# A quantised attention stage: 8-bit codes written as bytes into zeroed 16-bit words and multiplied as fp16, instead of codes raised by 1024 and copied to bf16

## The reference

```python
def _fq(x, delta, zp, n_bits):
    xi = round(x / delta) + zp
    xq = clip(xi, 0.0, 2.0 ** n_bits - 1.0)
    return (xq - zp) * delta
sim  = einsum('bhid,bhjd->bhij', _fq(q, dq, 128, 8), _fq(k, dk, 128, 8)) * SCALE
attn = softmax(sim, axis=-1)
out  = einsum('bhij,bhjd->bhid', _fq(attn, dw, 0.0, 8), _fq(v, dv, 128, 8))
```

## Time and profile before

| what | value |
|---|---|
| median of 3 runs | 1576.75 us |
| profiled execution, its own time | 1576.92 us |
| span of its records | 1575.1 us |
| VectorE busy | 1098.1 us |
| TensorE busy (matmul) | 1092.8 us |
| ScalarE busy | 894.2 us |
| GpSimd busy | 681.1 us |
| mean granted TensorE clock, share of full speed | 0.826 |

### The profile page before, as it was taken

One profiled execution on the slowest core, in us unless ns is written; L12 is line 12 of the kernel. 1 busy time (PEld: TensorE's weight loads), 2 busy tenths in 40 slices (PEclk: granted clock), 3 DMA queues, 4 the chain that ended last, 5 costly groups with the idle time before them and its releaser, 6 DMA issues.

```text
span 1575.1 us, 28607 instructions
## 1 busy us (share of the span) xinstructions
PE 1092.8 (69%) x9344; PEld 593.3 (38%) x9344; DVE 1098.1 (70%) x3102; ACT 894.2 (57%) x2546; POOL 681.1 (43%) x1055
## 2 busy tenths in 40 slices
PE   2888888887788797855353545444358778888888
PEld 1333344444333286831120212222225435453545
DVE  2687777777688653678888999877765666666522
ACT  1555554555554464567676797988852344646531
POOL 3321011011011416558888888877741344445310
PEclk9899999999999998975555555555569799999989
DMA  5213142101331112267555576665530121201000
GB/s 184 61 53 92 51 129 75 54 24 50 99 106 49 42 39 82 57 160 122 99 104 109 106 130 115 121 109 106 109 57 14 27 48 35 49 21 43 1 0 27
DMA packets 265219, 116.53 MB, mean 74 GB/s; under 512 B 216936, under 2 KB 253936, under 8 KB 262896
## 3 DMA queue, kind: packets, MB, share of 16 engines
q1 hardware_dynamic: 260112, 108.29, 30.8%
q0 software_dynamic: 2048, 4.20, 0.9%
q10 hardware_dynamic: 2912, 2.22, 0.5%
HBM read 38.80 MB, written 16.45 MB: 35 GB/s over the span
## 4 chain that ended last, share of the span: by engine, by line
PE 35%; POOL 21%; DVE 18%; issue 14%; ACT 9%; DMA 1%; SPq 0%; POOLq 0%; another core or an unknown queue 0%; ACTq 0%; DVEq 0%
POOL arena L2289 12%; ACT arena L1581 4%; PE acc L1199 3%; POOL inv_total L2278 2%; PE trans L1171 2%; DVE minus_top L1980 2%; PE misc L1021 2%; PE misc L1027 2%; PE trans L1323 2%; ACT arena L1528 2%; PE score L1335 2%; PE score L1337 2%; PE trans L1177 1%; POOL arena L2235 1%; PE acc L1385 1%
## 5 line engine op out<-in xcount | busy, mean ns | idle before, releaser
L2289 POOL TENSOR_SCALAR arena<-arena,inv_total 128x512 f16<-128x512 f32 (+1 forms) x512 | 299.7, 585 | 57.3 <-DVE inv_total L2058 16.8
L1980 DVE TENSOR_REDUCE minus_top<-score 128x4 f32<-128x616 f32 (+4 forms) x256 | 200.6, 802 | 95.3 <-PE score L1141 36.9
L2154 POOL TENSOR_TENSOR rstd<-spread,minus_half 128x4 f32<-128x4 f32 x36 | 37.5, 1043 | 489.5 <-DVE spread L1662 414.0
L1581 ACT ACTIVATE arena<-score,minus_top,exp_scale 128x512 f32<-128x512 f32 (+1 forms) x340 | 210.4, 625 | 20.9 <-POOL arena L2289 11.9
L1528 ACT ACTIVATE arena<-trans 128x512 f32<-128x512 f32 x240 | 134.4, 596 | 109.3 <-PE trans L1177 104.0
L1619 ACT ACTIVATE arena<-arena,minus_top 128x154 f32<-128x154 f32 x256 | 105.2, 412 | 129.3 <-DVE minus_top L2123 129.1
L1280 PE MATMUL score<-arena 32*128 32x512 bf16 (+1 forms) x340 | 68.9, 458 | 139.7 <-ACT arena L1581 138.7
L2064 DVE TENSOR_REDUCE top_score<-score 128x2 f32<-128x1024 f32 (+1 forms) x128 | 135.7, 1061 | 0.6 <-PE score L1280 0.5
L2309 POOL TENSOR_TENSOR arena<-arena,inv_total 128x512 f32<-128x512 f32 x64 | 66.5, 1040 | 143.9 <-DVE inv_total L2131 130.0
L1581 ACT ACTIVATE arena<-trans,minus_top,exp_scale 128x154 f32<-128x154 f32 (+1 forms) x172 | 105.5, 620 | 19.2 <-POOL arena L2289 14.9
L2118 DVE CUSTOM_DVE_ANT_0 arena<-score,arena 128x154 f32<-128x154 f32 x256 | 65.9, 313 | 60.6 <-PE score L1360 60.2
(11 more groups left out here) (283 smaller groups left out, 2814.4 us busy)
## 6 DMA issues: line engine op xcount, KB each, us to landing
arena<-q_terms SPq DMA_DIRECT2D x88, 128.0 KB, 2.8
late<-arena SPq DMA_DIRECT2D x128, 64.0 KB, 2.0
q_terms<-arena SPq DMA_DIRECT2D x36, 128.0 KB
late<-k_terms SPq DMA_DIRECT2D x32, 128.0 KB, 3.1
arena<-arena SPq DMA_TRANSPOSE x192, 3.1
by_expert<-zeros SPq DMA_DIRECT2D x2, 1472.0 KB, 9.8
arena<-by_expert SPq DMA_DIRECT2D x10, 256.0 KB
from_expert<-arena SPq DMA_DIRECT2D x10, 256.0 KB
```

The source lines that it names most:

```text
L1581: ins = nc.scalar.activation(probs[:, i % 3, j, of], quant_score[i % 3][:, j, of], ACT.Exp, bias=minus_top[:, at_col:at_col + 1], scale=ex ...
L1980: nc.vector.tensor_reduce(dst, src, axis=AX.X, op=ALU.max, negate=True).then_inc(top_ready, 1)
L2289: ins = nc.gpsimd.tensor_scalar(codes[:, (i - 1) % CODE_SOURCES, j, to], probs[:, (i - 1) % 3, j, of], inv_total[:, at_col:at_col + 1], HA ...
```

## The change

GpSimd no longer adds 1024 and no longer writes fp16. It writes the product alone, with an output type of unsigned byte, into every second byte of `codes`: the low half of each 16-bit word. The high halves are zeroed once, by a memset of the whole of `codes` before the first step of the stage; the memset waits until the last expert matmul is done, because `codes` lies on the experts' bytes. A 16-bit word with the value n in its low byte and zero above it is, read as fp16, n times 2^-24. The transposing DMA moves the 16-bit words as before, now straight into `pT_codes`, declared fp16. The VectorE pass `copy_codes`, its buffer name and its lag are gone, and TensorE waits for the two transposes themselves. The values `v_quant` are fp16 in place of bf16, so that both operands have one type, and `out_scale` takes back the factor 2^24.

```diff
-HALF_ROUND = 1024.0
+CODE_STEP = 2.0 ** -24
-QUANT_LAG, WEIGH_LAG, GROUPED_LAG = 6, 8, 2
+WEIGH_LAG, GROUPED_LAG = 8, 2
...
-        v_quant, v_quant_tail = put([P, 2, TILES, HEADS, 32], bf16), put([P, 2, HEADS, 32], bf16)
+        v_quant, v_quant_tail = put([P, 2, TILES, HEADS, 32], fp16), put([P, 2, HEADS, 32], fp16)
...
-        pT_codes = put([P, CODE_SLOTS, 2 * TILES, P], bf16)
-        put = place(arena, [pT_at])
-        pT_raised = put([P, CODE_SLOTS, 2 * TILES, P], fp16)
+        pT_codes = put([P, CODE_SLOTS, 2 * TILES, P], fp16)
...
+        code_bytes = codes.rearrange("p i j k -> p (i j k)").bitcast(mybir.dt.uint8)
+        code_bytes = code_bytes.rearrange("p (i j k b) -> p i j k b", i=CODE_SOURCES, j=2, b=2)[:, :, :, :, 0]
...
-                    nc.vector.tensor_scalar(out_scale[:, n:n + 1], vv, w, None, ALU.mult)
+                    nc.vector.tensor_scalar(out_scale[:, n:n + 1], vv, w, 1.0 / CODE_STEP, ALU.mult, ALU.mult)
...
-                    sp.dma_start_transpose(pT_raised[:, i % CODE_SLOTS, :, :],
+                    sp.dma_start_transpose(pT_codes[:, i % CODE_SLOTS, :, :],
...
-                    pe.wait_ge(codes_copied, 2 * n + 2)
+                    for i in (2 * n, 2 * n + 1):
+                        pe.wait_ge(codes_turned[i % CODE_SLOTS], 16 * (i // CODE_SLOTS + 1))
...
-                pe.wait_ge(codes_copied, len(QUANT_STEPS))
...
-                def copy_codes(i):
-                    of = i % CODE_SLOTS
-                    dve.wait_ge(codes_turned[of], 16 * (i // CODE_SLOTS + 1))
-                    nc.vector.tensor_scalar(pT_codes[:, of, :, :].rearrange("p k q -> p (k q)"),
-                                            pT_raised[:, of, :, :].rearrange("p k q -> p (k q)"),
-                                            -HALF_ROUND, 255.0, ALU.add, ALU.min).then_inc(codes_copied, 1)
...
-                    if QUANT_LAG <= i < quant_steps + QUANT_LAG:
-                        copy_codes(i - QUANT_LAG)
...
+                pool.wait_ge(down_raised, ALL_BLOCKS)
+                nc.gpsimd.memset(codes.rearrange("p i j k -> p (i j k)").bitcast(fp32), 0.0).then_inc(codes_cleared, 1)
+                pool.wait_ge(codes_cleared, 1)
...
-                                ins = nc.gpsimd.tensor_scalar(codes[:, (i - 1) % CODE_SOURCES, j, to], probs[:, (i - 1) % 3, j, of],
-                                                              inv_total[:, at_col:at_col + 1], HALF_ROUND, ALU.mult, ALU.add)
+                                ins = nc.gpsimd.tensor_scalar(code_bytes[:, (i - 1) % CODE_SOURCES, j, to], probs[:, (i - 1) % 3, j, of],
+                                                              inv_total[:, at_col:at_col + 1], None, ALU.mult)
```

More of the change, by code:

```diff
@@ L555, in build @@
         qT_codes, k4_codes = put([P, 2, TOKENS], bf16), put([P, 2, 4, TOKENS], bf16)
-        v_quant, v_quant_tail = put([P, 2, TILES, HEADS, 32], bf16), put([P, 2, HEADS, 32], bf16)
+        v_quant, v_quant_tail = put([P, 2, TILES, HEADS, 32], fp16), put([P, 2, HEADS, 32], fp16)
         probs = put([P, 3, 2, TOKENS])
-        pT_at = quant_at[0]
-        pT_codes = put([P, CODE_SLOTS, 2 * TILES, P], bf16)
-        put = place(arena, [pT_at])
-        pT_raised = put([P, CODE_SLOTS, 2 * TILES, P], fp16)
+        pT_codes = put([P, CODE_SLOTS, 2 * TILES, P], fp16)
         put = place(arena, [0])
         codes = put([P, CODE_SOURCES, 2, TOKENS], fp16)
+        code_bytes = codes.rearrange("p i j k -> p (i j k)").bitcast(mybir.dt.uint8)
+        code_bytes = code_bytes.rearrange("p (i j k b) -> p i j k b", i=CODE_SOURCES, j=2, b=2)[:, :, :, :, 0]
         put = place(arena, quant_at)
@@ L675, in build @@
         codes_ready = sem("codes_ready")
-        codes_copied = sem("codes_copied")
+        codes_cleared = sem("codes_cleared")
         pair_weighed = sem("pair_weighed")
```

## The result

The changed kernel takes 1767.26 us (median, 1760.61 to 1772.83) against 1575.06 for the kernel before: a ratio of 1.1219, 95% interval 1.1167 to 1.1271. It is slower, as forecast; the forecast of 1816 us was 49 us too high. The stated range of 1540 to 1846 us holds the measured time, but it was drawn wide enough to hold the faster cases too. The range that I gave to the slow case alone, 1790 to 1846 us, does not hold it.

What follows compares the result with a forecast made beforehand. GpSimd was taken to bound the self part and ScalarE the cross part; slower one-step code instructions gave +199.2 and +40.5 us, the end -0.5, so +239.2 on 1576.9: 1816 us, range 1540 to 1846.

Steps and rivals of the forecast that it cites:

- the faster cases: Quantised stage: one step costs as much as two, 1550 us, chance 0.36; or nothing is won, 1575 us, chance 0.05.
- the slow case: GpSimd's code instruction without a second step runs on a slower path: 1816 us, own range 1790 to 1846, chance 0.51.
- The bound: Quantised stage: GpSimd bounds the self part, 298.0 of 311 us; ScalarE paces the cross part, GpSimd about 20 us to spare.
- the sum: Quantised stage: self part +199.2 us, cross part +40.5, end -0.5, in all +239.2 on 1576.9, giving 1816 us.
- The form without a second step: GpSimd code instruction: one step costs 2.51 ns an element, so 1573 ns at 512 (from 721) and 674 at 154.
- the disturbed GpSimd instructions: Self part: without VectorE's copies GpSimd saves at most 7.4 us on code instructions and 5.9 us on L2278.
- The end of the stage: The last copy, 0.43 us, leaves the path from last transpose to last weighing: 0.5 us saved.
- VectorE's waits: In the quick one-step rival, half of the waits for VectorE go: self part -20 us in all, cross part -6.
- The memset: Ahead of the first reciprocal, from about 684.6 to 686.4 us: costs nothing; without that cover, 1.8 us.
- TensorE's waits at `weigh_pair`: Weighing: TensorE waits for transposes (a DMA) instead of copies; its wait can only end earlier.
- a quick one-step form: GpSimd code instruction: one step costs as much as two, 692 and 400 ns, giving 1550 us; chance 0.36.

Runs made afterwards that it cites:

- before_quarter: The kernel before, its code instruction adding 0.25 in place of 1024, copies on VectorE kept: 1572.81 us, ratio 0.9946.
- forms run: A program of its own timing thirteen GpSimd instruction forms, nothing else busy; at 512, bytes out: 1568 ns without a second step, 700 with an addition of zero.
- raised_no_copy: The changed kernel with fp16 numbers raised by 1024 in place of bytes, so the kernel before without the VectorE copy: 1565.85 us, ratio 0.9901.
- forms runs: Two programs of their own timing GpSimd instruction forms, the second varying the second step and output: start to start 767 ns adding 1024, 667 adding 0 or 0.25.

## Why the prediction was right, and which term was mis-sized

**The bound.** Right for what the sum needed, and too strong for the self part of the kernel before. With a slower code instruction GpSimd held both parts, and its waits vanished as the sum assumed: 4.1 us ahead of the first code work and none for another engine behind it. In the cross part before_quarter confirms that GpSimd had time to spare: with 100 ns less for each instruction it keeps its length, 160.3 us against 160.1. In the self part the same 26 us gave 9.6, so GpSimd held it together with VectorE, for whose maxima ScalarE waited 38.1 us there, against 26.1 us for GpSimd's codes. For a slowdown as large as this one that makes no difference; the price of a gain depends on it.

**The form without a second step.** Right, and the decisive step. Forecast 1573 and 674 ns from L2188 and L2278, measured 1571 and 687. The forms run showed why the row with bf16 could be trusted: input type is nothing here. The section of the Trainium skill that I had set against it (GPSIMD Engine Reference, section 3.1) puts a body of one or two operations for an element at 1.03 cycles; at the 1.2 GHz that the section reckons with this is an estimate of 0.86 ns. The traces agree for multiply-and-add, 0.82 ns for an element between 154 and 512 (400 and 692 ns), and do not for multiply alone, 2.47 ns (682 and 1568 ns), nor for multiply and maximum, 1998 ns at 512. Why GpSimd is slow without a second step, no run shows. That the bytes are not to blame the forms run shows: 1566 to 1570 ns for fp32, fp16 and bytes alike.

**The mis-sized term.** The sum added differences of recorded durations: 256 x 852 and 256 x 224 ns. I had kept the gap between two instructions as it was. In the kernel before, the next code instruction starts 73 ns (median) after the end of the last; in the changed kernel it starts 26 to 29 ns ahead of the recorded end, in the self and in the cross part. The steps show it. Before, the small instruction starts at 692.51 and 694.44, 1.93 us apart. After:

```profile
696.25 0.30 POOL L2272 TENSOR_SCALAR inv_total<-inv_total,inv_sizes 128x2 f32<-128x2 f32 x1
696.65 3.10 POOL L2284 TENSOR_SCALAR arena<-arena,inv_total 128x512 uint8<-128x512 f32 x2
699.72 0.30 POOL L2272 TENSOR_SCALAR inv_total<-inv_total,inv_sizes 128x2 f32<-128x2 f32 x1
```

3.47 us apart: +1.54, where two durations would give 2 x (1.565 - 0.692) = +1.75. About 100 ns too many in each of 512 instructions is 51 us, and the sum was 239.2 - 192.7 = 46.5 us too high in this stage. The other 5 us are two small misses the other way: the 154-wide instruction took 687 ns and not 674 (3.3 us), and L2278 fell by 33 ns and not 46 (1.7 us). The forms runs name the origin of that gap: it belongs to the constant 1024, whose instructions follow each other at 767 ns with a record of 692. By dropping the constant the change gave back what its record did not show.

**What the copies were worth.** For the disturbed GpSimd instructions I had priced 7.4 and 5.9 us; in raised_no_copy, with means of 707 and 300 ns, they come to 3.6 and 4.9, and the self part is 9.3 us shorter. The end of the stage, from the last code instruction to the last weighing, went from 4.2 to 3.8 us, 0.4 where I had put 0.5. Of VectorE's waits I had let half go as well, and that was too much: 16 us gained in all, not 26.

**The memset.** It started at 686.88, after a wait of 3.1 us for the last expert matmuls, took 1.80 us, and the first code work came at 692.76 after a further wait of 4.1 us: hidden, as forecast. TensorE's waits at `weigh_pair` passed from the copies to the transposes, 15.0 us in the whole stage, none of it on the path but at the end.

**The chances.** I gave 0.36 to a quick one-step form. Looking back, the rows pointed one way, but no row had the new form whole, and one row of bf16 carried the price at 512 by a straight line; the bare instruction, timed by itself, is what was missing.

## What to carry to other kernels

On GpSimd treat the removal of an arithmetic step as a change of form, not as a saving, and measure the form: here multiply alone took 1568 ns where multiply and add zero took 700. Take the cost of instructions on the bounding engine from start to start, for two with equal records of 692 ns differed by 100 ns there, and the kernel paid the difference. When a large edit loses, look for the one operand that can be given back: the design with a second step is worth 1.5%, of which 0.5% is the dropped constant, and with that step used for real work 2.4%.

## What the runs showed of the hardware that was not expected

- GpSimd, 512 fp32 elements, multiply by pointer and then: add a constant 692 to 703 ns, multiply by 1.0 686 to 692, multiply or add by pointer 762 to 779; nothing 1565 to 1572; maximum, minimum or subtract 1994 to 2012. Output as fp32, fp16, or bytes two apart is the same within 10 ns.
- One-step multiply by a constant instead of a pointer 1492 ns; a plain conversion fp32 to bytes two apart 617.
- Adding 1024 in place of 0 or 0.25 leaves the record at 692 to 703 ns and moves the next start from 667 to 767 ns. No cause is shown.
- TensorE multiplies fp16 codes of n x 2^-24 at the pace of bf16: the weighing matmuls of 128 columns, with weights 32 wide, have a mean of 307 ns in both kernels, at the granted clock of 0.50 to 0.51 of this stage.
